# An adaptive layer-norm block with sparse attention and experts: where queries, keys and values are projected, and in what widths

## The reference

```python
mod = (_silu(L0_c) @ L0_wmod).reshape(...)          # sa, ca, ga, sb, cb, gb
ga = (2 * (ga >= 0) - 1) * jnp.maximum(jnp.abs(ga), 0.25)     # gb alike
h = _layernorm(x, axis=-1) * (1 + ca) + sa
Q, K, V = proj(Wq, bq), proj(Wk, bk), proj(Wv, bv)  # of h: 32 heads x 2048 x 16
_, top_idx = jax.lax.top_k(norm(Q), 409)            # per head
out_sel = softmax(Q[top_idx] @ K.T * scale) @ V     # scattered back into zeros
x = x + ga * (out @ Wo.T + bo)
x = x + gb * experts(_layernorm(x) * (1 + cb) + sb) # top 2 of 8
```

## Time and profile before

| | us |
|---|---|
| median of 3 runs | 1120.99 (1120.28 to 1122.05) |
| the profiled execution | 1120.14 |
| its span, first to last instruction | 1118.3 |
| PE, DVE, ACT, Pool busy | 907.3, 879.3, 595.5, 581.5 |

### The profile page before, as it was taken

The page is one execution under the profiler, slowest core; times in us unless marked ns, Lnnn a source line. Parts: engine busy times, 40 slices in busy tenths (PEclk is TensorE's granted clock), DMA queues, the critical chain, the costliest instruction groups (busy, mean ns, idle before and its releaser), DMA issues. The chain is left out here.

```text
span 1118.3 us, 26572 instructions
## 1 busy us (share of the span) xinstructions
PE 907.3 (81%) x7725; PEld 569.2 (51%) x7726; DVE 879.3 (79%) x2070; ACT 595.5 (53%) x1351; POOL 581.5 (52%) x595
## 2 busy tenths in 40 slices
PE   7999300269999999999757722999999999999995
PEld 4444100212333333333346521877778888888884
DVE  4795688898999999997368876677787777777774
ACT  2565185308888888888534413544544444444441
POOL 2354374253777777763699821254454454545443
PEclk9999755557999999999889955999999999999998
DMA  7334673110111111120279812889943232323232
GB/s 244 105 128 155 221 232 119 28 42 20 25 39 24 38 24 40 30 73 23 75 208 263 253 33 59 240 225 219 225 90 48 48 47 47 52 42 53 41 48 29
DMA packets 125021, 110.55 MB, mean 99 GB/s; under 512 B 17489, under 2 KB 114449, under 8 KB 124945
## 3 DMA queue, kind: packets, MB, share of 16 engines
q1 hardware_dynamic: 102816, 86.76, 25.8%
q0 software_dynamic: 20480, 21.53, 11.8%
q10 hardware_dynamic: 1648, 1.31, 0.4%
HBM read 50.98 MB, written 35.50 MB: 77 GB/s over the span
## 5 line engine op out<-in xcount | busy, mean ns | idle before, releaser
L993 DVE TENSOR_REDUCE attend_mxh<-attend_p_a 128x1 f32<-128x512 f32 x416 | 258.6, 678 | 4.2 <-PE attend_p_a L1176 2.7
L1106 ACT ACTIVATE w<-attend_p_b 128x409 f32<-128x409 f32 x512 | 227.4, 515 | 44.1 <-PE attend_p_b L1190 43.4
L1914 ACT ACTIVATE expert_hr<-expert_p,b1t 128x256 f32<-128x256 f32 (+1 forms) x376 | 134.4, 423 | 194.0 <-PE expert_p L1852 177.5
L1807 POOL DMA_INDIRECT out_x<-expert_ys,expert_drop x72 | 121.6, 1689 | 191.9 <-DVE expert_ys L1949 133.4
L1874 PE MATMUL expert_p<-w,expert_hhi 128*128 x800 | 136.6, 273 | 0.5 <-DVE expert_ys L1949 0.3
L1852 PE MATMUL expert_p<-expert_xhi,w 128*128 128x256 f16 x800 | 136.4, 273 | 0.0
L1176 PE MATMUL attend_p_a<-w,attend_qa 64*128 64x512 f16 x384 | 123.2, 407 | 11.1 <-DVE attend_mxh L993 9.8
L1190 PE MATMUL attend_p_b<-attend_qb,w 64*128 64x409 f16 x512 | 130.4, 344 | 1.8 <-ACT w L1106 1.4
L918 POOL DMA_INDIRECT attend_qsel<-q_d,idx x96 | 91.5, 953 | 53.7 <-DVE attend_mxh L993 44.0
L1216 PE MATMUL attend_p_o<-w,attend_vh 128*32 128x409 f32 x1024 | 115.3, 523 | 0.7
L933 POOL DMA_INDIRECT attn_d<-outs,idx x90 | 89.1, 990 | 49.8 <-DVE attend_mxh L993 31.4
(11 more groups left out here) (350 smaller groups left out, 1770.7 us busy)
## 6 DMA issues: line engine op xcount, KB each, us to landing
expert_wu<-w SPq DMA_DIRECT2D x88, 256.0 KB
w<-in_L_ffn_w SPq DMA_DIRECT2D x20, 512.0 KB, 4.3
q_d<-project_q SPq DMA_DIRECT2D x32, 256.0 KB, 2.0
x<-in_L_attn_x SPq DMA_DIRECT2D x8, 512.0 KB, 10.1
attn_d<-zero SPq DMA_DIRECT2D x8, 512.0 KB
w<-k_d SPq DMA_DIRECT2D x32, 128.0 KB
route_ain<-attn_d SPq DMA_DIRECT2D x32, 128.0 KB
route_xin<-in_L_attn_x SPq DMA_DIRECT2D x32, 128.0 KB, 2.6
```

The costliest lines, as they stand in the source:

```text
L993: dve.tensor_reduce(mxh[q % 2][:, h, c, k:k + 1], p_a[chunk_use(q, a, h) % CB][:, :], AX, ALU.max).then_inc(a_done, 1)
L1106: act.activation(prob[:, 2 * (j % (TPB // 2)) + h, :], p_b[tile_use(p, j, h) % TB][:, 0:TOP], ACT.Exp, scale=SCALE / UNIT ** 2).then_inc(p ...
L1807: pool.indirect_dma_start(out=out, out_offset=bass.IndirectOffsetOnAxis(ap=drop[u][:, s:s + 1], axis=0), in_=ys[u][:, s, :], in_offset=Non ...
L1914: last = act.activation(hr[g % 2][:, f, rows], p_1[g][:, f, rows], ACT.Relu, bias=cst["b1t"][:, bass.ds(e[s] * FB + 2 * g + f, 1)], scale= ...
```

## The change

- Projection makes only the queries (256 columns, `wtq`). All normalised, turned tiles stay in memory (`ht`, 32 tiles), laid over expert weight space. Pool does `norm`; DVE keeps statistics, `y` and the sums. A query row is two slots, high and low (`HELD = 2`), each written once; Pool's memsets go. The modulation matmuls stand behind the turning of tiles 2, 4, 6 and 8. Values of the first four tiles follow the last tile.
- Selection: between the counting matmuls PE does one unit of keys and one tile of values, and more values between and behind the later counts. ACT, Pool and SP take the key units in turn with the weight pieces, three pieces to four units. The values are copied without bias by ACT. DVE waits for all values and key stores before `col1`, which overlays them.
- Attention: keys lie in another order of rows (high at 0 to 15, high and low at 16 to 47, the maximum's rows at 48 to 63), so that two slots give high, low, high: for the upper 32 rows a matmul of zeros (or of the maximum) goes first and the high part adds to it. `spread_v` adds the bias of V. The constants are loaded behind the keys; the modulation rows are finished by DVE at its end.

Its core:

```diff
-HELD = 4
+HELD = 2
...
-                def norm(t):
-
+                def ahead(t):
                     j, i = divmod(t, BLK)
-                    wait(dve, h_ps, t - R + 1)
-                    dve.wait_ge(rstd_done, j + 1)
-                    dve.tensor_scalar(h[t % R][:, :], x[:, t, :], mv[j % 2][:, i, 0:1], rstd[j % 2][:, i:i + 1], ALU.subtract, ALU.mult).then_inc(h_done, 1)
-                    if i == 1 and j + 1 < NB:
+                    if i == 0 and j + 1 < NB:
                         stats(j + 1)
-                    if i == 3 and j + 1 < NB:
+                    if i == 2 and j + 1 < NB:
                         invert(j + 1)
 
...
-                    dve.wait_ge(qv_ps, t + 1)
...
-                    dve.tensor_tensor(y[t % R][:, :], p_qv[t % 2][:, 0:D], biasb[:, b, 0:D], ALU.add).then_inc(y_done, 1)
-                    dve.tensor_tensor(cst["v"][:, t % TPB, b, :], p_qv[t % 2][:, D:2 * D], biasb[:, b, D:2 * D], ALU.add).then_inc(v_done, 1)
+                    dve.tensor_tensor(y[t % R][:, :], p_q[t % 2][:, 0:D], biasq[:, t // TPB, :], ALU.add).then_inc(y_done, 1)
...
-                unrolled([norm, None, None, None, evacuate, squares, modulation])
...
+                unrolled([ahead, None, None, evacuate, squares])
...
-                for i in range(8):
-                    pool.memset(q3[i][:, :, 2, :], 0.0).then_inc(gap_done, 1)
-                pool.wait_ge(gap_done, 8)
-                unrolled([None, None, None, None, None, second, None, last_of_block(second_k)])
+                    heads = y[t % R][:, :].rearrange("p (h d) -> p h d", h=H)
+                    pool.tensor_tensor(q3[t % 8][:, :, 1, :], heads, q3[t % 8][:, :, 0, :], ALU.subtract).then_inc(part1_done, 1)
+
+                def norm(t):
+
+                    j, i = divmod(t, BLK)
+                    wait(pool, h_ps, t - R + 1)
+                    pool.wait_ge(rstd_done, j + 1)
+                    pool.tensor_scalar(h[t % R][:, :], x[:, t, :], mv[j % 2][:, i, 0:1], rstd[j % 2][:, i:i + 1], ALU.subtract, ALU.mult).then_inc(h_done, 1)
+
+                unrolled([norm, None, None, None, second])
...
+                    act.activation(ht[:, :, t, :], p_h[t % 2][:, 0:D].rearrange("p (k n) -> p k n", k=KD), ACT.Copy).then_inc(ht_done, 1)
+                    if t in MOD_AT:
+                        i = MOD_AT.index(t)
+                        act.wait_ge(mod_ps, i + 1)
+                        act.activation(mod[:, i // 2, (i % 2) * 512:(i % 2 + 1) * 512], p_mod[i % 2][:, :], ACT.Copy).then_inc(mod_done, 1)
...
-                    act.activation(q3[t % 8][:, :, 0:2, :], y[t % R][:, :].rearrange("p (h d) -> p h d", h=H).unsqueeze(2).broadcast_to([P, H, 2, HD]), ACT.Copy).then_inc(part0_done, 1)
+                    act.activation(q3[t % 8][:, :, 0, :], y[t % R][:, :].rearrange("p (h d) -> p h d", h=H), ACT.Copy).then_inc(part0_done, 1)
...
                     for k in range(KD):
-                        last = pe.matmul(p_qv[t % 2][:, :], ht[t // BLK % 2][:, k, t % BLK, :], wtb[:, t // TPB, k, 0:2 * D], start=(k == 0), stop=(k == KD - 1))
-                    last.then_inc(qv_ps, 1)
...
+                        last = pe.matmul(p_q[t % 2][:, 0:D], ht[:, k, t, :], wtq[:, t // TPB, k, :], start=(k == 0), stop=(k == KD - 1))
+                    last.then_inc(qy_ps, 1)
+
+                unrolled([turn_h, None, project])
+                for m in range(V_FIRST):
...
-                pe.wait_ge(cst["rows_here"], 16)
...
@@ -605,21 +537,33 @@
                     sp.dma_start(attn[c], cst["zero"][:, 0:W].unsqueeze(1).broadcast_to([P, NT // CLEARS, W])).then_inc(cleared, 16)
                 for i in range(8):
                     sp.wait_ge(cst["q_saved"][i], 16 * NT // 8)
+                sp.dma_start(io["q3_d"][B * L * H:, :], cst["zero"][:, 0:HELD * HD // 2].bitcast(F16)).then_inc(spare_saved, 16)
+
+                def load(i):
+                    wait(sp, wlo_done, i - WR + 1)
+                    sp.dma_start(raw_tile(wraw[i % WR], i), raw_of(io, i)).then_inc(w_here[i % WR], 16)
+
+                def save(u):
+                    b, l0 = divmod(u // 2 * KT, L)
+                    n0 = b * H + u % 2 * (P // HD)
+                    sp.wait_ge(klo_done, u + 1)
+                    for r in range(PARTS):
+                        sp.dma_start(io["k3_d"][n0:n0 + P // HD, r, :, l0:l0 + KT], k3[u % 2][:, r, :]).then_inc(k_saved[u % 2], 16)
+
+                for i in range(WR):
+                    load(i)
+                loads = itertools.count(WR)
+                for u in range(UNITS_K):
+                    save(u)
+                    if u % 4 != 3:
+                        load(next(loads))
+                for i in loads:
+                    if i >= WLAST:
+                        break
+                    load(i)
...
+
+                def low_key(u):
+                    pool.wait_ge(yk_done, u + 1)
+                    pool.wait_ge(khi_done, u + 1)
+                    pool.tensor_tensor(k3[u % 2][:, 1, :], yk[u % 2], k3[u % 2][:, 0, :], ALU.subtract).then_inc(klo_done, 1)
+
+                weights = itertools.count(WFIRST)
+                for u in range(UNITS_K):
+                    low_key(u)
+                    if u % 4 != 3:
+                        low_weight(next(weights))
+                for i in weights:
...
+                def high_key(u):
+                    bias = bkb[:, u % 2, u // 2 * KT // L:u // 2 * KT // L + 1]
+                    act.wait_ge(k_ps, u + 1)
+                    wait(act, klo_done, u - 1)
+                    act.activation(yk[u % 2], p_k[u % 2][:, :], ACT.Identity, bias=bias).then_inc(yk_done, 1)
+                    wait(act, k_saved[u % 2], 16 * PARTS * (u // 2))
+                    act.activation(k3[u % 2][:, 0, :], p_k[u % 2][:, :], ACT.Identity, bias=bias).then_inc(khi_done, 1)
+
+                def values(m):
+                    b, i = divmod(2 * m, TPB)
+                    act.wait_ge(v_ps, m - V_FIRST + 1)
+                    act.activation(cst["v"][:, i:i + 2, b, :], p_v[m % 2][:, :, :], ACT.Copy).then_inc(v_done, 1)
+
+                weights = itertools.count(WFIRST)
+                for u in range(UNITS_K):
+                    high_key(u)
+                    if u % 4 != 3:
+                        high_weight(next(weights))
+                    if u % 2:
+                        values(V_FIRST + u // 2)
+                pairs = itertools.count(V_FIRST + UNITS_K // 2)
+                for i in weights:
+                    if i >= WLAST:
+                        break
+                    for m in itertools.islice(pairs, 2):
+                        if m < NT // 2:
+                            values(m)
+                    high_weight(i)
...
+
+                def keys(u):
+
+                    j, oc = divmod(u, 2)
+                    b = j * KT // L
+                    wait(pe, yk_done, u - 1)
+                    wait(pe, khi_done, u - 1)
+                    for k in range(KD):
+                        last = pe.matmul(p_k[oc][:, :], wtkv[:, b, k, D + oc * P:D + (oc + 1) * P], ht[:, k, 4 * j:4 * j + 4, :].rearrange("p t n -> p (t n)"),
+                                         start=(k == 0), stop=(k == KD - 1))
+                    last.then_inc(k_ps, 1)
+
+                def values(t):
+
+                    m, i = divmod(t, 2)
+                    if i == 0:
+                        wait(pe, v_done, m - V_FIRST - 1)
+                    for k in range(KD):
+                        last = pe.matmul(p_v[m % 2][:, i, :], ht[:, k, t, :], wtkv[:, t // TPB, k, 0:D], start=(k == 0), stop=(k == KD - 1))
+                    if i:
+                        last.then_inc(v_ps, 1)
+
+                tiles = itertools.count(2 * V_FIRST)
+                keys(0)
+                values(next(tiles))
                 for i in range(PAIRS):
                     pe.wait_ge(cnt_done, i + 1)
                     pe.matmul(p_c[:, 0:3], same[:, :], cnt[:, 0:3], start=True, stop=True).then_inc(cnt_ps, 1)
+                    keys(i + 1)
+                    values(next(tiles))
                 pe.wait_ge(cnt_done, PAIRS + 1)
                 pe.matmul(p_c[:, 0:1], same[:, :], cnt[:, 0:1], start=True, stop=True).then_inc(cnt_ps, 1)
+                for t in itertools.islice(tiles, 2):
+                    values(t)
                 pe.wait_ge(cnt_done, PAIRS + 2)
                 pe.matmul(p_c[:, 0:1], same[:, :], cnt[:, 0:1], start=True, stop=True)
                 pe.matmul(p_c[:, 1:2], before[:, :], cnt[:, 1:2], start=True, stop=True).then_inc(cnt_ps, 1)
+                for t in itertools.islice(tiles, 4):
+                    values(t)
                 pe.wait_ge(cnt_done, PAIRS + 3)
                 pe.matmul(p_c[:, 2:3], before[:, :], cnt[:, 0:1], start=True, stop=True).then_inc(cnt_ps, 1)
+                for t in itertools.islice(tiles, 3):
+                    values(t)
...
+                dve.wait_ge(v_ps, NT // 2 - V_FIRST)
+                for i in range(2):
```

(24 more changed lines are left out.)

261 lines of the change are left out of this document (103 added, 158 removed).

## The result

The changed kernel takes **1134.07 us** (median of 4, 1130.71 to 1137.09) beside 1121.52 us of the kernel before: ratio 1.0113, 95% interval 1.0097 to 1.013. It is slower, where I had forecast 1088.7 us and faster. The profiled execution took 1135.07 us, its span 1133.3, 15.0 more than before.

The account below looks back on a forecast made before the run. It took PE to bound the projection and a DVE-PE chain the selection. Projection -48.2, rounds +11.9, tail +3.0 and attention +1.0 gave -32.3 from 1120.14 us, plus 0.85 for the median: 1088.7 us, range 1077 to 1109.

Parts of the forecast that it names:

- Attention, +1: Attention stage: added small matmuls cost 0 to +5 us, taken as +1; Pool's bias addition hidden by its idle share.
- Projection, -48.2: Projection: Pool bounds tiles at 1.41 us each, so selection starts at 77.3 instead of 125.53 us.
- the two clauses: Skill text on Pool's elementwise speed: norm 0.73 us by the two-input clause, 0.37 by the one-input clause.
- The modulation's +4: Projection: modulation matmuls of 7.1 us, now between tiles 2 and 9, lengthen the stage by 4 us.
- Rounds, +11.9: Selection rounds: count 16 comes at 63.4 us into the stage instead of 51.5, with ACT as bound.
- The stall: Early selection: ACT waits for its first weight piece until 17.6 us into the stage, PE idle around 10 us.
- rival 4: Selection: PE's clock stays low, 1.2 GHz, through the rounds, +33 us; 1121 us, no change; chance 0.03.
- rival 2: Selection: key stores become the bound of the rounds, +11 us; 1100 us; chance 0.13.
- Tail, +3.0: Selection's end: ACT, done at 80.7 us, is wanted at 76.5; 4.2 less 1.2 slack costs 3.0 us.
- 1: Projection: Pool's normalising costs 0.905 us, +9.6 us in all; 1098 us; chance 0.15.
- 3: First weight piece lands 5 to 7 us sooner, Pool's norm at 0.31 gains 3 in projection; 1079 us; chance 0.08.
- 5: PE's low clock holds in the projection too, +28 us there, modulation +7; 1156 us; chance 0.04.

Follow-up runs that it names:

- v_copy: Changed kernel with Pool's plain copy for spreading the values in the attention, bias of V left out: 1117.77 us, ratio 0.9965.
- moves_reduce: Changed kernel with the three small DVE copies per pair of heads written as a maximum over one element: 1106.78 us, ratio 0.9876.
- clears_between: Changed kernel with the first four weight loads first and the eight clearing writes between the key stores: 1132.85 us, ratio 1.0117.
- norm_dve: Changed kernel with the normalising of the rows on DVE again instead of Pool: 1127.94 us, ratio 1.0077.
- mod_late: Changed kernel with the modulation matmuls behind tiles 12, 16, 20 and 24: ratio 1.0027 at the lower clock.
- before_reduce_fourth: Kernel before the change with its three small DVE copies per pair of heads written as maxima, at clock 1.00: 1111.40 us, ratio 0.9909.
- combined_again: Changed kernel with norm on DVE, clearing writes between key stores, four key buffers and copies as maxima; second run, lower clock: ratio 0.9736.
- combined_third: Changed kernel with norm on DVE, clearing writes between key stores, four key buffers and copies as maxima; third chip, lower clock: ratio 0.9744.
- combined: Changed kernel with norm on DVE, clearing writes between key stores, four key buffers and copies as maxima; first run, lower clock: ratio 0.9733.
- key_bufs: Changed kernel with clearing writes between the key stores and four key buffers instead of two: ratio 0.9909 at the lower clock.
- The four repairs: Changed kernel with norm on DVE, clearing writes between key stores, four key buffers and copies as maxima, at clock 1.00: 1080.86 us, ratio 0.9635.
- pool_forms: Changed kernel with Pool's norm in four forms, one per tile of each four: 0.92 to 1.22 us per operation, 2.3 to 3.1 times the copy.

## Why the prediction was wrong

The sum was -32.3; the span showed +15.0. The 47.3 between them, by its steps:

- **Attention, +1, "hidden by Pool's idle share": +22.0, so 21.0 off, the largest.** This is the step that failed. I priced Pool's longer operation by Pool's idle time. What mattered was who waits for Pool while it runs. DVE was full (its idle time is a few us), so each wait of DVE is the kernel's. The trace of before had the sign of it, a copy of 25 x 2 elements with a mean of 466 ns where 160 do, and I read no row of it. Shown by v_copy (18.6 us from Pool's operation) and moves_reduce (all of it from DVE's form). That the short falls of the clock follow from the starved PE is argued from their order, seen five times in after and seven times in clears_between; that they vanish with the long waits is what v_copy and moves_reduce show.
- **Projection, -48.2: -32.0, so 16.2 off.** Pool's norm, 0.60 us, took 1.24. Even my upper bound, 0.905, was too low, since it came from another operation, and so were the 0.37 and 0.73 by the two clauses that the prediction cites. A copy prices no `tensor_scalar` there. The 31 steps from the first low part to the last took 58.0 us where 31 x 1.41 + 4 are 47.7: 10.3 of the 16.2, and norm_dve took 10.8 away. Another 5.6 are the start: the first low part was ready at 31.85 us instead of 26.2. I had sent one tile through alone; in PE's queue the turning of the third tile, behind three norms of 1.24 us, and a modulation group of 3.22 us at the low clock stand ahead of the first query matmul. The modulation's +4 fits the steps behind that (4.0), but leaves out this first delay, 2.0 us by mod_late.
- **Rounds, +11.9: +18.6, so 6.7 off.** 1.4 of it is a reading: the matmul at 130.51 was the first of the 15 and the last round is short, so count 16 of before came at 50.1 us, not 51.5. The stall was right to 0.6 us. But count 4 came at 26.9 instead of 24: PE came out of its 11.14 us of idle time at the low clock, with 3.75 us for the keys and 1.91 for the values, so rival 4 was true for one round. The last 2.4 are the twelve rounds behind it, 3.48 us each instead of 3.3. "I take 0" for the key stores was wrong, ACT waited 8.1 us for them (rival 2). And ACT's own pace was taken too slow: its operations start before the recorded end of the one ahead, 0.57 us apart for keys recorded at 0.685, and with four buffers the rounds ran at 3.09.
- **Tail, +3.0: +6.5, so 3.5 off.** ACT's spreads began 3.8 us after DVE had their input ready, as I said, but they end at 197.37, and DVE's last one, 1.15 us, at 199.90: ACT alone would have held it only until 198.5. What ends last is DVE, whose operations with two inputs got slower beside Pool's weight pieces: L755 took 1.53 us and L759 2.44, 0.69 each before, and of L777 two took some 2.6 us each while Pool had its last two pieces, all others 0.68. The prediction has no term for that; it is read from one trace each, and no run tests it.
- **Right:** Pool as the bound of the projection; the modulation's operations hidden at the attention's end; the added matmuls between 0 and 5 us (3.4 in v_copy, none to be seen between moves_reduce, 318.9, and before_reduce_fourth, 320.3). At the lower clock the attention is longer than in the kernel before with the same three lines by some 8, 7 and 4 us on three chips (combined_again 405.8 against 397.4, combined_third 407.8 against 400.9, combined 409.5 against 405.6). That these are the added matmuls is likely, but Pool's addition differs there too.
- **Rivals.** 1 was true beyond its price (1.24 us, not 0.905), 2 in part: the twelve rounds took 2.4 us more than at the forecast's pace, 4.7 more than at the 3.09 of key_bufs. 3 and 5 didn't come, 4 in one round only. None of them lay in the attention.

The four repairs end below the forecast, at 1080.86 us, and not by its path: about 9 us are the copies' cost in the kernel before, and the norm is on DVE. The stage with the selection still starts at 83.78, not at 77.3.

## What to carry to other kernels

Lengthening an operation on an idle engine is free only if nobody waits for it while it runs: look for tiny operations of the full engine whose mean is several times their minimum. Price an operation on an engine by the same operation there, not by a copy; where the trace has none, the range must be wide enough to say so. And work moved into the waits of a chain needs buffers for its slowest follower, a store's landing included.

## What the runs showed of the hardware

- A DVE copy between memory tiles was held beside Pool's addition, up to 1.98 us for 25 x 2 elements (0.16 alone, 0.67 at most beside Pool's copy); as a maximum over one element it takes 0.145 us beside the same addition. The copy shown above began 0.49 us ahead of the recorded start of Pool's addition; what held it then, the transfer issue before it or a rough record, is open.
- Pool, 128 x 256 in single precision: copy 0.40 us, `tensor_scalar` 0.92 with one operand of the row, 1.08 with two constants, 1.22 with two operands of the row (pool_forms). DVE: 0.40 for the last (norm_dve).
- A DVE operation with two inputs, 128 x 512, took 0.68 us alone and some 2.6 while Pool subtracted on 128 x 1024 (L777 in after).
- The clock in the attention was 1.00 on some chips and 0.86 to 0.90 in the mean, by falls to 0.50, on others, and with it DVE was full or waited for PE: the changed kernel is 1.1% slower than before on the one, 0.4% on the other, and in the kernel before the same three lines are worth 9 us or 2 to 6.
